# Second pass of a two-layer kernel: the sign flip of the words' low halves moved from VectorE's 32-bit XOR to a 16-bit subtraction on GpSimd

## The reference

```
# layer 0: a Clifford-algebra product over groups of 8x8 values
x = x + _L0_conv_ref(_gn(x), L0_conv_weight, L0_conv_bias)
# layer 1
x = x + _L1_conv_ref(_gn(x), ...)

def _L1_conv_ref(x, conv_w, ...):
    res = x
    h = _batchnorm(x, bn1_gamma, bn1_beta)          # statistics over all images
    h = sign(h)
    bw = sign(conv_w) * scale_per_output_channel
    h = conv3x3(h, bw, padding 1, 16 groups)        # 32 channels to 32
    h = _batchnorm(h, bn2_gamma, bn2_beta)          # statistics over all images
    h = h + res
    return where(h > 0, h, prelu_a * h)
```

## Time and profile before

| | |
|---|---|
| median of three runs | 4704.78 us |
| the profiled execution's own time | 4701.64 us |
| its span in the trace | 4699.4 us |
| PE busy | 4509.8 us, 96% |
| DVE busy | 4235.9 us, 90% |
| ACT busy | 3861.5 us, 82% |
| POOL (GpSimd) busy | 1478.8 us, 31%, nothing of it in pass 2 |
| DMA | 1612.17 MB, mean 343 GB/s |
| pass 2 in the trace | first pack at 1763.9 us, last `unpack` at 2858.4 us |

### The profile page before, as it was taken

One profiled execution on the slowest core, in us unless ns is written; L12 is line 12 of the kernel. 1 busy time (PEld: TensorE's weight loads), 2 busy tenths in 40 slices (PEclk: granted clock), 3 DMA queues, 4 the chain that ended last, 5 costly groups with the idle time before them and its releaser, 6 DMA issues.

```text
span 4699.4 us, 83432 instructions
## 1 busy us (share of the span) xinstructions
PE 4509.8 (96%) x21948; PEld 2748.6 (58%) x22204; DVE 4235.9 (90%) x10523; ACT 3861.5 (82%) x5517; POOL 1478.8 (31%) x3481
## 2 busy tenths in 40 slices
PE   6999999999999979999999996999999999999999
PEld 6999999999999974433333332444444444444444
DVE  6999999999999989999999997888888888888887
ACT  7999999999999967777777774777777777777776
POOL 4888888888888880000000000000000000000000
PEclk9999999999999999999999998999999999999999
DMA  5888888888888879999999996999999999999998
GB/s 202 318 317 316 318 319 318 317 318 320 321 317 317 317 282 351 370 369 368 368 368 368 369 368 252 377 375 376 374 376 375 376 377 374 377 375 375 376 376 297
DMA packets 686229, 1612.17 MB, mean 343 GB/s; under 512 B 30002, under 2 KB 423986, under 8 KB 620658
## 3 DMA queue, kind: packets, MB, share of 16 engines
q1 hardware_dynamic: 686194, 1611.76, 95.0%
HBM read 940.55 MB, written 671.10 MB: 343 GB/s over the span
## 4 chain that ended last, share of the span: by engine, by line
PE 76%; POOL 6%; ACT 6%; issue 5%; DVE 5%; DMA 1%; SPq 0%; DVEq 0%; POOLq 0%; ACTq 0%
PE psV L1007 13%; PE psT L1066 12%; PE psV L1066 12%; PE psT L1082 8%; PE psT L1084 7%; PE psV L1084 7%; PE psV L1082 7%; PE psT L990 7%; DVE ring_x L952 4%; ACT ring_y L675 3%; PE psV L1004 3%; POOL ring_y L481 2%; ACT ring_g L584 1%; POOL u_r L495 1%; POOL x_r L457 1%
## 5 line engine op out<-in xcount | busy, mean ns | idle before, releaser
L1007 PE MATMUL psV<-W0T,ring_gT 128*128 128x128 f32 x8192 | 1080.0, 275 | 47.6 <-issue 34.0
L1007 PEld LDWEIGHTS psV<-W0T,ring_gT 128*128 128x128 f32 x8192 | 1076.8, 192 | 33.6
L770 DVE BATCH_NORM_STATS2 early<-ring_z 128x6 f32<-128x128 f32 x4096 | 822.7, 274 | 0.0
L761 DVE SCALAR_TENSOR_TENSOR ring_z<-psV,x_r,ring_x 128x1024 f32<-128x1024 f32 x512 | 657.2, 1284 | 117.3 <-DVE early L770 76.9
L665 ACT ACTIVATE late<-ring_x,minus_b 128x512 f32<-128x512 f32 x1024 | 639.5, 707 | 1.3 <-PE psV L1084 1.3
L632 ACT ACTIVATE ring_x<-ring_x,bn_c 128x1024 f16<-128x1024 f32 x512 | 604.2, 1229 | 31.0 <-DMA bn_c<-bn_scratch 31.0
L850 DVE BATCH_NORM_STATS2 h_tup<-ring_x 128x6 f32<-128x512 int16 x1024 | 619.4, 668 | 0.0
L481 POOL TENSOR_SCALAR ring_y<-ring_z,u_r,u_nm 128x1024 f32<-128x1024 f32 x512 | 605.8, 1199 | 35.6 <-POOL gn L500 35.6
L964 DVE SCALAR_TENSOR_TENSOR ring_x<-ring_x,bn_q,psV 128x512 f32<-128x512 f32 x512 | 376.1, 744 | 255.2 <-PE psV L1084 254.9
L590 ACT ACTIVATE ring_g<-ring_x,x_ms 128x1024 f32<-128x1024 f32 x512 | 585.3, 1143 | 0.0
L675 ACT ACTIVATE ring_y<-ring_y,gnb 128x512 f32<-128x512 f32 x512 | 368.0, 801 | 239.7 <-DVE ring_x L952 202.3
(11 more groups left out here) (150 smaller groups left out, 5857.6 us busy)
## 6 DMA issues: line engine op xcount, KB each, us to landing
ring_x<-in_x SPq DMA_DIRECT2D x128, 2048.0 KB, 8.8
y_scratch<-ring_y SPq DMA_DIRECT2D x128, 2048.0 KB, 12.7
ring_x<-y_scratch SPq DMA_DIRECT2D x512, 512.0 KB, 6.2
out<-ring_x SPq DMA_DIRECT2D x256, 1024.0 KB, 14.0
h_scratch<-ring_x SPq DMA_DIRECT2D x256, 512.0 KB, 6.1
ring_y<-y_scratch SPq DMA_DIRECT2D x128, 1024.0 KB, 7.3
ring_z<-y_scratch SPq DMA_DIRECT2D x128, 1024.0 KB, 7.4
ring_g<-h_scratch SPq DMA_DIRECT2D x64, 1024.0 KB, 11.6
```

The source lines that it names most:

```text
L761: dve.scalar_tensor_tensor(out=ring_z[:, c % 2, cols], in0=psV[:, j % 2, :], scalar=x_r[:, s, j:j + 1], in1=ring_x[:, s, cols], op0=ALU.mu ...
L770: last = dve.bn_stats(z_tup[:, s, j, 2 * r:2 * r + 2, :].rearrange("p h t -> p (h t)"), ring_z[:, c % 2, SL * j + 2 * S * r:SL * j + 2 * S ...
L1007: last = pe.matmul(psV[:, j % 2, P * r:P * (r + 1)], ring_gT[:, j, P * r:P * (r + 1)], W0T[:, :], start=False, stop=(r % 4 == 3))
```

## The change

GpSimd gets a new function `flip` and a new semaphore. For each tile it waits until `unpack` has written the words, and then adds -32768 to the low half of each word: it reads 1024 unsigned 16-bit numbers that lie 4 bytes apart, and writes 1024 signed 16-bit numbers to the same places. DVE's `flip` and its calls go away. What waited for `flipped` (the store on SP, `h_stat` on DVE) waits for it still, and its count is now raised by GpSimd.

```
@@ gpsimd
             last.then_inc(diag_done, 1)
+
+            def flip(i, c):
+
+                pool.wait_ge(unpacked, SLOTS * i + c + 1)
+                pool.sem_inc(flip_begun)
+                halves = [word_slot(c % SLOTS).bitcast(kind).rearrange("p (f e) -> p e f", e=2)[:, 0] for kind in (I16, U16)]
+                pool.tensor_scalar(halves[0], halves[1], -float(HALF16), None, ALU.add).then_inc(flipped, 1)
+
+            rounds(pool, flip, T2, 2 * HEAD)
+
             pool.wait_ge(bn2_step, BN2_VE)
@@ vector
-            def flip(i, c):
-
-                dve.wait_ge(unpacked, SLOTS * i + c + 1)
-                words = word_slot(c % SLOTS)
-                dve.tensor_scalar(words, words, HALF16, None, ALU.bitwise_xor).then_inc(flipped, 1)
-
             def pass2(i, c):
-                if from_round(i, c, 3):
-                    flip(i, c - 3)
                 if from_round(i, c, 8) and c % J == 0:
@@
             last = (T2 - SLOTS) // SLOTS
-            for c in range(1, SLOTS):
-                flip(last, c)
             for c in range(SLOTS):
```

More of the change, by code:

```diff
@@ L14 @@
 I16 = mybir.dt.int16
+U16 = mybir.dt.uint16
 P = 128
@@ L255, in two_layer_kernel @@
         unpacked = sem("unpacked")
+        flip_begun = sem("flip_begun")
         flipped = sem("flipped")
```

## The result

The changed kernel takes 4686.13 us (median of 6 runs, 4683.92 to 4687.15), the kernel before 4703.24 us beside it (6 runs, 4701.56 to 4704.99). The ratio is 0.9963, with a 95% interval of 0.9950 to 0.9975: faster by 17.1 us. Forecast were 14.7 us of gain and 4690 us. The measured time is 3.9 us under the forecast and lies at the lower end of its range (4686). The interval leaves 12 to 24 us of gain, so single microseconds can't be told apart from the times alone. The profiled execution has a span of 4682.1 us, against 4699.4 before, so the two traces differ by 17.3 us, and in them I look for the difference.

A forecast was written before the change was run, and what follows sets the result against it. DVE was taken to bound PE for 85% of pass 2, by 0.068 us a tile. The pace gives 14.7 us, the end of pass 2 counts 0: 4704.8 - 14.7 = 4690 us, range 4686 to 4695.

The forecast's parts named there:

- PE's own pace as the bound: Pass 2: without DVE's flips, PE sets the pace at 4.205 us for a tile, in place of 4.27.
- 14.7 us from the pace: Pass 2: tile 255 starts at 2839.3 at PE's own pace instead of 2853.97, a gain of 14.7 us.
- The end of pass 2, counted as 0: Behind the last tiles: DMA sets the stretch from pass 3's loads on, so moving the flips gains 0 us.
- sum of 2.4 us from a convolution's end to its flip's end: End of pass 2, tile 252: on GpSimd 0.1 + 1.0 + 0.1 + 1.2 = 2.4 us, against 3.1 on DVE.
- D, the flip's duration: GpSimd's flip of one tile in pass 2: between 0.7 and 3.2 us, taken as 1.2.
- Pack and flip take turns: Pass 2: DVE's pack and GpSimd's flip block each other in full; a flip up to 3.0 us disturbs nothing.
- the first rival: Pass 2: a slow flip of 3.23 us alternates with pack, 4.43 us for a tile, 4747 us in all; chance 0.22.
- the lock: Pass 2: a pack or flip that comes later waits until the other engine's whole instruction is over.
- DVE's list, 3.68 us: Pass 2: without the flip of 0.59 us, DVE needs 4.27 - 0.59 = 3.68 us for a tile.
- pack waits for PE by 0.5 us in each tile: Pass 2: expected profile sign that DVE's pack waits for PE by 0.5 us or more in each tile.
- DMA allows the pace: Pass 2: the DMAs can move the 374 GB/s that 4.205 us for a tile needs, at no cost.
- the second rival: Pass 2: DMA sustains only 370 GB/s, 4.25 us for a tile, gain 3 us, 4702 us; chance 0.10 including partial loss.

The follow-up runs named there:

- half_flip: The kernel before, with the flip still on DVE but of only the first 512 of a tile's 1024 words: 4685.34 us, ratio 0.9962.
- late_loads: The changed kernel, with SP waiting for the convolution of tile 254 before it issues the loads of pass 3: 4688.51 us.
- two_ops: The changed kernel, with GpSimd's flip written as two operations, times 1.0 and then plus -32768: 4684.55 us.
- extra_read: The changed kernel, with one more GpSimd instruction behind each flip that reads, doubles and writes 128 float32 numbers: 4697.89 us.
- extra_write: The changed kernel, with a GpSimd memset of 512 16-bit numbers behind each flip, which reads no SBUF: 4695.33 us.
- two_ops_b: The same kernel as two_ops, the changed kernel with a two-operation flip on GpSimd, timed again: 4684.85 us, ratio 0.9961.

## Why the prediction came out as it did

- **PE's own pace as the bound: right.** 4.205 us was predicted and 4.205 measured, to the end of the pass. half_flip shows that the bound is PE's pace and not the length of the flip taken off.
- **14.7 us from the pace: right**, 14.6 us by the weight loads of tile 254 (14.4 by the rows of matmuls). That nothing took the gain away again was in part luck, as the point on pack and flip below says.
- **The end of pass 2, counted as 0: wrong, and this is the term that was missed.** It gave 2.96 us. The prediction said rightly that DMA sets this stretch from the loads' issue on, and that the loads wait for the flip of tile 252. Its error was in what that flip waits for. It put it 3.1 us behind its convolution's end at 2849.7. But that is the end of tile 253's convolution. The flip of 2852.11 is of tile 252, whose unpack had been over since 2845.63 + 1.02 = 2846.65:

```profile
2845.63 1.02 ACT L643 ACTIVATE ring_x<-psT 128x1024 int32<-128x1024 f32 x1 [0.98 <-PE psT L1066]
```

So for 5.5 us it had stood in DVE's list, which ran behind PE, after the statistics of tile 251. On GpSimd it starts at once and ends at 2832.53 + 3.06 = 2835.59, P + 0.27, against P + 3.07 before: 2.8 us, and late_loads, which holds the loads back, loses the gain again. A DVE whose list is short enough does as well: in half_flip the flip ends at P + 0.2. The prediction's own sum of 2.4 us from a convolution's end to its flip's end was nearly right (2.7 us in two_ops, whose flip takes 1.35); it was set against the wrong tile. Of the 3.9 us by which the time came below the forecast the missed term is nearly 3; 1.5 is that the kernel before has a median of 4703.24 in the newer runs and not 4704.8; the rest, half a microsecond the other way, is less than what the medians can tell.
- **D, the flip's duration: 1.2 us taken, 3.07 measured.** The row of the same element count, L481, is a two-operation instruction, and two_ops shows that the second operation makes the instruction short. The row of one operation, L553, was the right one: its slope gave 3.23. The count of operations in the row should have decided, and not the count of elements.
- **Pack and flip take turns: wrong, and so the forecast was lucky.** With the measured D, the first rival has 1.2 + 3.07 = 4.27 us for a tile, as in the kernel before, and no gain in the middle of the pass. By its own rule, then, the prediction should have lost the 14.7 us. That the size D was missed did no harm, because a second error made up for it: the lock is not there for this pack. It starts inside running flips and takes 1.23 to 1.45 us, 2.07 in the one worst case, and never the rest of a 3 us flip on top. The evidence for the lock was a float32 addition, which was carried over to the float16 pack. What tells the held instructions from the others isn't shown: h_keep is float32 and is held, but the aggregates are float32 too and take 179 ns in the mean in both kernels, though most of them run beside a flip now. Of the Trainium skill's rule ("SBUF — State Buffer", § Who interferes with whom), by which an instruction with two SBUF inputs and one of GpSimd that reads block each other in full, the runs bear out one direction only, GpSimd behind the pack (4.09 for 3.08 us). The Trainium skill's "roughly line-rate" for one input ("GPSIMD Engine Reference", § 4.1 Engine selection) fits the flip with two operations, 1.35 us, and not the one with a single operation, 3.07.
- **DVE's list, 3.68 us: 4.03 measured.** Parts of the difference are in the rows: waits for its own results (19.0 + 12.3) / 233 = 0.13 us for a tile; h_keep (0.644 - 0.158) / 4 = 0.12; and the last of the statistics is seen to its end, 2.42 for 2.34, where the flip had overlapped it. That makes 4.01 us. The claim that pack waits for PE by 0.5 us in each tile was wrong for that reason: at most 0.45, and in half of the tiles none.
- **DMA allows the pace: right**, 374 GB/s; the second rival did not come about.

## What to carry to other kernels

When work is taken off an engine's list, its price comes back only down to the next bound, here PE, 0.07 us away; and what it covered, waits of the engine for its own results, comes into sight. Look at what stands in front of the stage's last stores and loads: an engine that is behind delays them as well, and when it catches up, the stage's end gets shorter too, here by 3 us beside the 14.6 of the pace. Before work goes to a free engine, ask whether shortening it on the old one reaches the same bound: here 0.27 us off DVE's list was enough (half_flip, which leaves out a part of the result, only measures this). A load issued earlier can cost more than it gives when stores stand behind it. When the price of an instruction is read from another row, take the row with the same number of operations and the same form before the one with the same size.

## What the runs showed of the hardware

- GpSimd's tensor_scalar with one operation takes 3.07 us for 1024 numbers in each partition, with two operations (a product and a sum) 1.35 us. Between 128 (593 ns) and 1024 numbers the single one costs 2.8 ns a number.
- A running GpSimd instruction delays DVE's float16 scalar_tensor_tensor with two SBUF inputs by 0 to 0.22 us (1.45 for 1.23) in all tiles but one, and by 0.84 us once (2.07), when both began together. It holds a float32 tensor_scalar of 16 numbers until the instruction's end (0.64 us in the mean for 0.16, 1.02 with the extra read on GpSimd). In the other direction GpSimd's instruction grows by nearly the rest of the pack: 4.09 us for 3.08, with 1.15 us of the pack to go.
- A DVE instruction that waits for the statistics issued just before it loses 0.21 us in the changed kernel (0.33 in one tile of four of extra_read and extra_write); one that waits for a small tensor_scalar 0.33.
- The 16 DMA engines don't always finish a batch together: of one and the same program, one profile had them end evenly (two_ops), and in the other (two_ops_b) a share of 0.1 to 0.4 ran on for 1.2 us.
